# A top-two mixture of experts on TensorE: the down products two experts behind the up products, and the routing of the next batch in three parts

## The reference

```
x = x + tanh(g_ffn[3]) * ffn(layernorm(x))

def ffn(x):                                  # E, K, D, H = 8, 2, 128, 256
    scores = softmax(x @ gate_w.T)           # 8 scores for each row
    top_scores, sel = top_k(scores, 2)
    # each row: sum over its two experts e of
    #   score[e] * ((silu(x @ w1[e]) * (x @ w3[e])) @ w2[e])
```

## Time and profile before

| | |
|---|---|
| profiled execution, whole | 1411.15 us |
| its span | 1409.4 us |
| mean granted TensorE clock | 0.929 |
| PE busy | 1243.8 us (88%) |
| PE weight loads busy | 861.1 us (61%) |
| DVE busy | 822.8 us (58%) |
| ACT busy | 640.4 us (45%) |
| POOL busy | 576.3 us (41%) |

### The profile page before, as it was taken

How to read it: one execution, slowest core, us unless ns; L and a number is a source line. 1 busy time by engine, 2 the same in 40 slices (tenths; PEclk the granted TensorE clock), 3 DMA queues, 4 the chain that set the end, 5 groups by cost and what they waited for, 6 DMA issues and landing times.

```text
span 1409.4 us, 26279 instructions
## 1 busy us (share of the span) xinstructions
PE 1243.8 (88%) x9595; PEld 861.1 (61%) x9595; DVE 822.8 (58%) x2600; ACT 640.4 (45%) x1310; POOL 576.3 (41%) x1098
## 2 busy tenths in 40 slices
PE   6998755899999969998899989989989899989897
PEld 3444223367778734554788744436877477878786
DVE  5788287555444257883566578753555443465654
ACT  1677453355554436774222247764223554332332
POOL 4343273866763486630434444442223783000000
PEclk9999755999999968999999969998999999999999
DMA  4000000000000040000000000003000000000001
GB/s 133 11 1 2 1 1 0 1 1 1 1 1 2 0 134 1 2 2 1 2 0 0 1 1 2 2 2 132 2 1 1 1 1 2 1 1 0 0 0 31
DMA packets 15335, 16.84 MB, mean 12 GB/s; under 512 B 6403, under 2 KB 12564, under 8 KB 14582
## 3 DMA queue, kind: packets, MB, share of 16 engines
q1 hardware_dynamic: 15222, 15.34, 3.5%
HBM read 14.28 MB, written 1.05 MB: 11 GB/s over the span
## 4 chain that ended last, share of the span: by engine, by line
PE 36%; DVE 6%; POOL 5%; issue 3%; ACT 2%; DVEq 0%; POOLq 0%; ACTq 0%
PE banks L3073 6%; PE banks L2455 4%; PE banks L3081 4%; PE banks L2203 3%; PE banks L2481 2%; PE banks L2819 2%; PE banks L2193 2%; PE banks L519 1%; PE banks L2790 1%; PE banks L558 1%; PE banks L2804 1%; PE banks L2866 1%; DVE x_resident L2146 1%; DVE f_hiddenT L3014 1%; PE banks L2464 1%
## 5 line engine op out<-in xcount | busy, mean ns | idle before, releaser
L533 DVE TENSOR_REDUCE x_minus_max<-banks 128x2 f32<-128x512 f32 x256 | 169.8, 686 | 53.1 <-PE banks L519 51.8
L541 ACT ACTIVATE x_probs<-banks 128x512 f32<-128x512 f32 x256 | 151.7, 600 | 89.6 <-PE banks L525 88.4
L519 PE MATMUL banks<-x_kT,x_qT 32*128 32x256 bf16 x512 | 103.2, 302 | 19.7 <-DVE x_minus_max L533 10.6
L3073 PE MATMUL banks<-xnT,w_f_w 128*128 128x256 f32 x512 | 119.8, 379 | 0.0
L525 PE MATMUL banks<-x_qT,x_kT 32*128 32x256 bf16 x512 | 98.7, 291 | 2.2 <-ACT x_probs L541 1.7
L3073 PEld LDWEIGHTS banks<-xnT,w_f_w 128*128 128x128 f32 x512 | 93.0, 190 | 10.3
L3048 ACT ACTIVATE f_gate<-banks 128x512 f32<-128x512 f32 x64 | 38.2, 597 | 127.6 <-PE banks L3073 127.6
L1806 DVE CUSTOM_DVE_ANT_0 x_work<-banks,hide_later_keys 128x128 f32<-128x128 f32 (+1 forms) x256 | 79.9, 352 | 26.6 <-PE banks L1919 25.0
L3014 DVE TENSOR_TENSOR f_hiddenT<-banks,f_gate 128x512 f32<-128x512 f32 x64 | 44.0, 688 | 70.9 <-ACT f_gate L3048 70.4
L3081 PE MATMUL banks<-w_f_w,f_hiddenT 128*128 128x128 f32 x512 | 69.6, 279 | 15.1 <-DVE f_hiddenT L3014 15.1
L1850 ACT ACTIVATE x_work<-banks 128x384 f32<-128x384 f32 x128 | 62.6, 495 | 42.2 <-PE banks L1925 41.4
(11 more groups left out here) (513 smaller groups left out, 3083.4 us busy)
## 6 DMA issues: line engine op xcount, KB each, us to landing
w_f_w<-in_f_w SPq DMA_DIRECT2D x5, 1024.0 KB, 7.0
out<-x_resident SPq DMA_DIRECT2D x1, 1024.0 KB, 5.2
x_resident<-in_x SPq DMA_DIRECT2D x1, 896.0 KB, 6.0
context_rows<-in_ctx SPq DMA_DIRECT2D x1, 768.0 KB, 5.0
contextT<-in_ctxT SPq DMA_DIRECT2D x1, 672.0 KB, 8.1
w_f_wg<-in_f_wg SPq DMA_DIRECT2D x1, 544.0 KB, 4.9
w_f_wu<-in_f_wu SPq DMA_DIRECT2D x1, 544.0 KB, 5.8
w_f_wd<-in_f_wd SPq DMA_DIRECT2D x1, 512.0 KB, 6.0
```

The costliest lines, as they stand in the source:

```text
L519: mm = nc.tensor.matmul(K.PS[:, SMAX0 + m % 2, t * S:(t + 1) * S], h["qT"][r, c % 3, g, t * P:(t + 1) * P], h["kT"][r, c % 3, g, :], start ...
L533: K.nc.vector.tensor_reduce(h["nm"][:, b % 2, :, n], K.PS[:, SMAX0 + n % 2, :].rearrange("p (t n) -> p t n", t=T), AX_X, ALU.max, negate=T ...
L541: K.nc.scalar.activation(h["p"][:, n % (2 * HG)], K.PS[:, ST0 + n % 2, :], ACT.Exp).then_inc(s["p"].sem, 1)
L3073: mm = nc.tensor.matmul(K.PS[:, 2 * (e % 2) + k, c * S:(c + 1) * S], W[name][:, e * HE3 + c * P:e * HE3 + (c + 1) * P], K.norm["xnT"][:, u ...
```

## The change

- `carried_pipeline` takes the place of `software_pipeline`: batch 0 in straight code, batches 1 to 6 in the loop, two to a body, batch 7 in straight code. `main` gets the batch before as well.
- PE runs down(e-2) behind up(e). The last two down products of a batch come behind up(0) and up(1) of the next; behind the last batch both follow at the end. up(e) now waits for h of e-2 (which also says that the banks have been read), and down(e) waits for the adds of e-2, which have read its output bank.
- DVE: mul(e) now waits also for down(e-2), which has read the half of `f_hiddenT` that it writes. Behind it comes add(e-2), over batch ends too.
- The preparation of a batch on DVE: statistics after expert 0, rows after 1, the negated maximum after 3 (before: 4), and the rest of the routing in three parts after experts 5, 6 and 7. The wait for the last adds of a batch stands only behind the last batch.
- ACT: the exponentials stand behind silu(4) instead of silu(7).

```diff
+def carried_pipeline(eng, prep, main):
+    main(0, 0, None, prep(1, 1))
+    with eng.Fori(0, B // 2 - 1) as i:
+        main(2 * i + 1, 1, 2 * i, prep(2 * i + 2, 0))
+        main(2 * i + 2, 0, 2 * i + 1, prep(2 * i + 3, 1))
+    main(B - 1, 1, B - 2, None)
...
 # vector, prep
             for t in range(T):
                 nc.vector.max(top[:, t], sc[:, t]).then_inc(chain.sem, 1)
                 chain.next()
+            if in_parts:
+                yield
...
             for sh, dst in ((1, ca), (2, cb), (4, ca)):
+                if sh == 4 and in_parts:
+                    yield
...
 # vector, main
             for e in range(NE3):
                 dve.wait_ge(s["g"].sem, s["g"].after(b, e + 1))
+                if e >= 2:
+                    dve.wait_ge(s["down_ps"].sem, s["down_ps"].after(b, e - 1))
+                elif before is not None:
+                    dve.wait_ge(s["down_ps"].sem, s["down_ps"].after(before, NE3 + e - 1))
                 nc.vector.tensor_tensor(hT[:, e % 2].rearrange("p c n -> p (c n)"), K.PS[:, 2 * (e % 2) + 1, :], g[:, e % 2], ALU.mult) \
                     .then_inc(s["h"].sem, 1)
-                if e >= 1:
-                    add_expert(e - 1)
-                if e in (0, 1, 4):
+                if e >= 2:
+                    add_expert(b, u, e - 2)
+                elif before is not None:
+                    add_expert(before, 1 - u, NE3 + e - 2)
+                if e in (0, 1, 3, 5, 6, 7):
                     next_stage(stages)
-            add_expert(NE3 - 1)
-            dve.wait_ge(ending.sem, ending.reached())
-            next_stage(stages)
...
 # scalar, main
-                if e in (2, 7):
+                if e in (2, 4):
                     next_stage(stages)
...
 # tensor, main
             def up(e):
+                if e >= 2:
+                    pe.wait_ge(s["h"].sem, s["h"].after(b, e - 1))
+                elif before is not None:
+                    pe.wait_ge(s["h"].sem, s["h"].after(before, NE3 + e - 1))
...
-            def down(e):
-                pe.wait_ge(s["h"].sem, s["h"].after(b, e + 1))
+            def down(b, e, before):
+                if e >= 2:
+                    pe.wait_ge(s["main_step"].sem, s["main_step"].after(b, (e - 1) * T))
+                elif before is not None:
+                    pe.wait_ge(s["main_step"].sem, s["main_step"].after(before, (NE3 + e - 1) * T))
...
                 up(e)
                 if e in (2, 3):
                     next_stage(stages)
-                if e >= 1:
-                    down(e - 1)
-            down(NE3 - 1)
+                if e >= 2:
+                    down(b, e - 2, before)
+                elif before is not None:
+                    down(before, NE3 + e - 2, None)
+            if stages is None:
+                for e in (NE3 - 2, NE3 - 1):
+                    pe.wait_ge(s["h"].sem, s["h"].after(b, e + 1))
+                    down(b, e, before)
```

More of the change, by code:

```diff
@@ L2948, in vector, with prep @@
     def vector(dve):
-        chain, ending = Chain(s["prep_step"]), Chain(s["main_step"])
-        def prep(b, u):
+        chain, added = Chain(s["prep_step"]), s["main_step"]
+        def prep(b, u, in_parts=True):
             chain.start(b)
@@ L2998, in prep, with main, add_expert @@
             yield
-        def main(b, u, stages):
-            ending.start(b)
-            def add_expert(e):
+        def main(b, u, before, stages):
+            def add_expert(b, u, e):
                 dve.wait_ge(s["down_ps"].sem, s["down_ps"].after(b, e + 1))
                 if e > 0:
-                    dve.wait_ge(ending.sem, ending.reached())
+                    dve.wait_ge(added.sem, added.after(b, e * T))
                 for t in range(T):
                     x = K.X[:, bass.ds(b * S + t * P, P)]
-                    nc.vector.scalar_tensor_tensor(x, K.PS[:, OUT0 + e % 2, t * D:(t + 1) * D], wt[:, u, t, e:e + 1], x, ALU.mult, ALU.add).then_inc(ending.sem, 1)
-                    ending.next()
+                    nc.vector.scalar_tensor_tensor(x, K.PS[:, OUT0 + e % 2, t * D:(t + 1) * D], wt[:, u, t, e:e + 1], x, ALU.mult, ALU.add).then_inc(added.sem, 1)
             for e in range(NE3):
                 dve.wait_ge(s["g"].sem, s["g"].after(b, e + 1))
+                if e >= 2:
+                    dve.wait_ge(s["down_ps"].sem, s["down_ps"].after(b, e - 1))
+                elif before is not None:
+                    dve.wait_ge(s["down_ps"].sem, s["down_ps"].after(before, NE3 + e - 1))
                 nc.vector.tensor_tensor(hT[:, e % 2].rearrange("p c n -> p (c n)"), K.PS[:, 2 * (e % 2) + 1, :], g[:, e % 2], ALU.mult) \
                     .then_inc(s["h"].sem, 1)
-                if e >= 1:
-                    add_expert(e - 1)
-                if e in (0, 1, 4):
-                    next_stage(stages)
-            add_expert(NE3 - 1)
-            dve.wait_ge(ending.sem, ending.reached())
-            next_stage(stages)
-        yield from placed(prep(0, 0), (0, 2, 6, 8))
-        software_pipeline(dve, prep, main)
+                if e >= 2:
[3 more added lines that the diff above has]
+                if e in (0, 1, 3, 5, 6, 7):
+                    next_stage(stages)
+            if stages is None:
+                add_expert(b, u, NE3 - 2)
+                add_expert(b, u, NE3 - 1)
+                dve.wait_ge(added.sem, added.after(b))
+        yield from placed(prep(0, 0, False), (0, 2, 6, 8))
+        carried_pipeline(dve, prep, main)
     def gpsimd(pool):
@@ L3032, in gpsimd @@
         yield from placed(prep(0, 0), (1,))
-        software_pipeline(pool, prep, lambda b, u, stages: all_stages(stages))
+        carried_pipeline(pool, prep, lambda b, u, before, stages: all_stages(stages))
     def scalar(act):
@@ L3048, in main @@
                 nc.scalar.activation(g[:, e % 2], K.PS[:, 2 * (e % 2), :], ACT.Silu).then_inc(s["g"].sem, 1)
-                if e in (2, 7):
+                if e in (2, 4):
                     next_stage(stages)
         yield from placed(prep(0, 0), (4, 7))
-        software_pipeline(act, prep, main)
+        carried_pipeline(act, prep, main)
     def tensor(pe):
@@ L3088, in main @@
                     next_stage(stages)
-                if e >= 1:
-                    down(e - 1)
-            down(NE3 - 1)
+                if e >= 2:
+                    down(b, e - 2, before)
+                elif before is not None:
+                    down(before, NE3 + e - 2, None)
+            if stages is None:
+                for e in (NE3 - 2, NE3 - 1):
+                    pe.wait_ge(s["h"].sem, s["h"].after(b, e + 1))
+                    down(b, e, before)
         yield from placed(prep(0, 0), (3, 5))
-        software_pipeline(pe, prep, main)
+        carried_pipeline(pe, prep, main)
     return Programs(s, gpsimd, vector, scalar, tensor)
```

## The result

| | before | after | ratio (95% interval) |
|---|---|---|---|
| first comparison, median | 1407.49 us | 1391.58 us | 0.9874 (0.9839 to 0.9909) |
| the same program again, median | 1406.21 us | 1390.15 us | 0.9870 (0.9836 to 0.9905) |
| profiled execution, whole | 1411.15 us | 1390.70 us | |
| its span | 1409.4 us | 1388.9 us | |
| last FFN, first up product to last add | 192.29 us | 176.45 us | |

The ratios leave out slow executions where there were any; they are estimates of their own and not the quotients of the medians beside them, which are 0.9887 and 0.9886. The medians fell by 15.9 and 16.1 us; 15.3 was forecast. The last FFN alone, measured in the trace from its first up product (1211.05 before, 1206.48 after) to the end of its last add (1402.73 + 0.61 before, 1382.93 after), lost 15.84 us.

What follows compares the result with a forecast made beforehand. TensorE bounds the last FFN, apart from 2.53 us stalls at batch ends. 6 x (21.62 + 0.40) + 20.96 + 4.09 = 157.2 us against 172.3; with 0.2 from batch 0, gain 15.3: 1408.32 becomes 1393.0 us, range 1391 to 1396.

Steps and rivals of the forecast that it cites:

- What bounds the stage: Last FFN: TensorE at its own rate is the bound in mid-batch; only batch ends make it wait for VectorE.
- the stalls of 2.5 us a batch: Batch ends, TensorE: 0.79 us lost at down(7) waiting for h, 1.74 at down(0) behind VectorE's routing chain; 2.53 us together.
- From mark to mark: Last FFN, up(7) of batch 0 to down(7) of batch 7: 157.2 us forecast against 172.3 before.
- the loss at the transposes: TensorE behind up(2): next batch's normalised rows come late, 0.40 us taken per batch, bounds 0.3 and 0.7, six times.
- the drain: Behind the stage's last up(7): down(7) waits for expert 5's adds and starts near 4.09 us after it.
- lag behind a down product: VectorE's gated product mul(e), waiting for down(e-2), was taken to start 1.09 us after that down product starts.
- New waits at nothing: TensorE, ahead of up and down groups in the loop: a wait already met was taken to cost 0.
- The table switch in mid-batch: ScalarE, exponentials behind silu(4): silu(5) at 5.6 us after up(4) instead of 4.55, hidden with 0.9 us left before up(7).
- The first rival: ScalarE: table switch holds it twice its load, 1.8 us in each of seven batches, whole time 1405.5 us; chance 0.04.
- The routing in three parts: VectorE: chain of 3.33 us cut into 1.00, 1.05 and 1.28 behind adds of experts 5, 6, 7; all hidden.
- The reason given for the order: Down products two behind: both batch-end waits go, and up(e+2) has 1.7 us of slack where the old order had about 1.
- a microsecond for the medians: Whole kernel time: allowance for scatter of medians in the forecast's range, beside 0 to 0.7 us for the transposes.

Runs made afterwards that it cites:

- order alone: Changed kernel with its order of down products kept but the routing back where it was, behind silu(7) and expert 7: stage 188.16 us, whole median 1407.5 us.
- routing alone: Kernel before with only the routing in three parts and exponentials behind silu(4), down products unchanged: stage 180.44 us, whole median 1395.1 us.

## Where the prediction was right, and where it failed

**What bounds the stage, and the stalls of 2.5 us a batch.** Right, and the two causes named were separable: order alone 4.1 us, routing alone 11.9, sum 16.0, together 15.8.

**From mark to mark.** Forecast 157.2 us from up(7) of batch 0 to the last down(7); measured 1381.15 - 1224.37 = 156.8. In its terms: the loss at the transposes 0.31 us a batch instead of 0.40 (0.5 us in all), the drain 4.25 instead of 4.09, batch 0 0.26 us shorter (17.89 from up(0) to up(7), before 18.15) instead of 0.2. The lag behind a down product was met: 1.09 us in most places of the loop, 1.16 in the last batch, which is part of the longer drain. The gain of the stage, 15.84, is 0.5 more than forecast.

**New waits at nothing.** Right: two more in front of every up product changed the stage by 0.01 us.

**The table switch in mid-batch.** silu(5) was forecast at 5.6 us after up(4); 1222.08 - 1216.51 = 5.57. The first rival is out: the stage's traces show no hold, neither ahead of exponentials nor ahead of a silu of 512 columns, and four loads within 6 us take 1.28 us each. The Trainium skill ("ScalarE: Activation LUTs", "What ACT_TABLE_LOAD costs") gives a drain of about 1.38 us beside the load for each switch; here the trace disagrees. That the cover is thin was right too: with 3 us more in the same place all of the gain is gone.

**The routing in three parts.** Hidden, as forecast. In one piece it costs 8.1 us.

**The reason given for the order.** Here the argument was too kind to the change. I credited the distance of two with its slack and took the price, mul(1) bound to down(7), only as what is late next. The runs show that the distance of one, carried over batch ends, does as well: it was the carrying and the routing that brought the gain. Inside the loop the second expert of distance makes no difference beyond 0.1 us a batch, and it adds 0.9 us at the end of the stage.

**The step that failed: from the stage to the whole time.** The mechanism was right and so was the stage. What failed is the last term, "a microsecond for the medians", and with it the base that it was added to, the median of three runs, 1408.32. These three and a fourth have the median 1407.49, thirteen later ones 1406.21, so the base was 0.8 to 2.1 us too high. From these, less the 15.84 us of the stage, 1391.65 and 1390.37 follow, and the measured medians are 1391.58 and 1390.15. The eight times of the changed kernel lie between 1388.82 and 1395.39 us, 3.8 above to 2.8 below the first median. With a forecast of 1393.0 the low end of 1391 left 2 us below it for base, scatter and stage together. By the first comparison's ratio, 0.9874 of 1407.49, the changed kernel is at 1389.8, below the range, with an interval of 4.9 us to either side; the median of its runs, 1391.58, is in it, and that of the second comparison, 1390.15, is below. The three runs known before and their profiled execution were already 4.5 us apart (1406.65 to 1411.15). A profiled execution 2.8 us above the median should have been read as such a scatter, not as a constant offset. That the scatter comes from the granted clock is seen in single executions (0.50 against 1.00 at 155 to 165 us, 4.6 us; 0.50 against 0.77 at 930 to 960); that all of it does is not shown.

## What to carry to other kernels

Where TensorE is the bound and only pauses at the ends of batches, list the waits at one end separately, and give each its own edit: carrying the last product over the end and moving the side chain into the slots each removed its own stall, and neither did the other's. Cut a side chain into pieces that are shorter than the slack of the slots they go into. Test the distance between producer and consumer by itself: here one and two were within 1.1 us of each other, the larger one put a wait of its own into the path, and moving one piece of work into that wait removed it. When a gain of one per cent is to be measured, measure the stage in the trace and not the whole.

## What the runs showed of the hardware

Behind a pause of 2.0 us of TensorE, at the same place of each of seven batches, the granted clock fell in two (0.86 and 0.80, then 0.87 and 0.79, over two stretches of 5 us) and stayed at 1.00 in the others. In the kernel before it stayed at 1.00 through the whole stage, whose pauses were 0.5 to 1.9 us. Ahead of the stage it fell to 0.50 at 155 us of one execution and not at 155 to 165 of another of the same code. 96 semaphore waits of TensorE against a register, all met, changed the stage by 0.01 us. A table load of ScalarE takes 1.28 us and the next activation starts 0.01 to 0.02 us behind it.
